# A gated cross-attention and expert layer: GpSimd's subtraction for the next batch behind the means and factors, and one gate product a step earlier

## The reference, cut to what matters

```python
xn, ln = layernorm(ctx), layernorm(layernorm(x))        # media and latents
q = ln @ Wq + bq;  k, v = split(concat(xn, ln) @ Wkv + bkv)   # 8 heads of 128
attn = softmax(q @ k.T * 128 ** -0.5)                  # 256 rows x 512 keys
x = x + tanh(g_xattn) * (attn @ v @ Wo + bo)
xh = layernorm(x)
gates = xh @ Wg + bg                                   # 8 experts, the top 2 by softmax
x = x + tanh(g_ffn) * sum over the top 2 of w_e * (silu(xh @ W1[e] + b1[e]) @ W2[e] + b2[e])
```

## Time and profile before

| | |
|---|---|
| three runs | 1504.64, 1505.71 (median), 1506.18 us |
| the profiled execution, its own time | 1498.99 us |
| its span, first to last instruction | 1497.3 us |
| TensorE busy | 1464.5 us, 98% of the span |
| VectorE busy | 1223.7 us, 82% |
| ScalarE busy | 942.0 us, 63% |
| GpSimd busy | 580.1 us, 39% |
| TensorE clock | at full speed but for the last of 40 slices |

### The profile page before, as it was taken

One profiled execution on the slowest core, in us unless ns is written; L12 is line 12 of the kernel. 1 busy time (PEld: TensorE's weight loads), 2 busy tenths in 40 slices (PEclk: granted clock), 3 DMA queues, 4 the chain that ended last, 5 costly groups with the idle time before them and its releaser, 6 DMA issues. The chain is left out here.

```text
span 1497.3 us, 29981 instructions
## 1 busy us (share of the span) xinstructions
PE 1464.5 (98%) x10138; PEld 1345.8 (90%) x10138; DVE 1223.7 (82%) x3169; ACT 942.0 (63%) x2047; POOL 580.1 (39%) x650
## 2 busy tenths in 40 slices
PE   8999999999999999999999999999999999999997
PEld 6888888888888888888988888988899999999996
DVE  7879989898898989989898998787767766666685
ACT  5665655656556555655656556556668877777775
POOL 4323324242332424324243333333444555445542
PEclk9999999999999999999999999999999999999998
DMA  6210101101110110101101010032556555555563
GB/s 200 57 36 15 43 22 41 53 16 43 23 36 22 51 43 15 44 22 46 48 16 44 23 36 22 8 98 70 111 153 195 157 132 134 145 145 128 132 184 76
DMA packets 83491, 107.99 MB, mean 72 GB/s; under 512 B 24297, under 2 KB 68390, under 8 KB 83086
## 3 DMA queue, kind: packets, MB, share of 16 engines
q1 hardware_dynamic: 67374, 87.03, 18.2%
q0 software_dynamic: 15824, 18.98, 7.9%
q10 hardware_dynamic: 144, 0.05, 0.0%
HBM read 87.68 MB, written 18.35 MB: 71 GB/s over the span
## 5 line engine op out<-in xcount | busy, mean ns | idle before, releaser
L973 POOL TENSOR_SCALAR probs<-probs,rsum 128x512 f32<-128x512 f32 x256 | 182.4, 724 | 636.2 <-DVE rsum L1696 630.1
L1197 ACT ACTIVATE pt_hi<-turn 128x512 fp32r<-128x512 f32 x256 | 139.0, 595 | 228.3 <-PE turn L1356 226.8
L999 POOL DMA_INDIRECT out_rows<-yo,token x71 | 127.6, 1797 | 188.5 <-DVE yo L1872 168.6
L1821 DVE TENSOR_TENSOR ht_lo<-hs,ht_hi 128x512 fp32r<-128x512 f32 x142 | 98.3, 692 | 116.1 <-ACT ht_hi L1164 112.9
L1096 ACT ACTIVATE probs<-score,nbias 128x512 f32<-128x512 f32 x256 | 172.8, 684 | 1.9 <-DVE nbias L1692 1.8
L1155 ACT ACTIVATE hs<-ph,vecs 128x256 f32<-128x256 f32 (+1 forms) x284 | 114.2, 457 | 94.5 <-PE ph L199 84.1
L1948 DVE TENSOR_TENSOR pt_lo<-turn,pt_hi 128x512 fp32r<-128x512 f32 x256 | 164.0, 682 | 3.9 <-ACT pt_hi L1197 3.5
L1690 DVE TENSOR_REDUCE smax<-score 128x1 f32<-128x512 f32 x256 | 164.0, 679 | 2.9 <-PE score L199 2.7
L197 PE MATMUL py<-w_hi,ht_lo 128*128 (+1 forms) x568 | 162.8, 287 | 3.2 <-DVE ht_lo L1821 1.7
L198 PE MATMUL py<-w_lo,ht_hi 128*128 (+1 forms) x568 | 161.0, 284 | 0.6 <-issue 0.5
L199 PE MATMUL py<-w_hi,ht_hi 128*128 (+1 forms) x568 | 160.8, 283 | 0.0
(11 more groups left out here) (251 smaller groups left out, 4746.5 us busy)
## 6 DMA issues: line engine op xcount, KB each, us to landing
w_raw<-in_L_ffn_W SPq DMA_DIRECT2D x45, 1024.0 KB, 5.4
spread<-mean_and_factor SPq DMA_DIRECT2D x15, 512.0 KB
xhat_rows<-rows SPq DMA_DIRECT2D x16, 264.0 KB, 2.2
x_raw<-in_x SPq DMA_DIRECT2D x16, 256.0 KB, 3.0
c_raw<-in_ctx SPq DMA_DIRECT2D x16, 256.0 KB, 3.2
out_rows<-x SPq DMA_DIRECT2D x16, 256.0 KB
z_turned<-in_x_turned SPq DMA_DIRECT2D x15, 256.0 KB, 3.8
z_turned<-in_ctx_turned SPq DMA_DIRECT2D x15, 256.0 KB, 4.5
```

Source lines behind the costliest of these rows:

```text
L973: last = pool.tensor_scalar(probs[n % 2][:, t, :], probs[n % 2][:, t, :], rsum[:, n % 2, t:t + 1], 1.0, ALU.mult, ALU.mult)
L999: pool.indirect_dma_start(out=A["out"], out_offset=bass.IndirectOffsetOnAxis(ap=token[:, u:u + 1].bitcast(U32), axis=0), in_=yo_of(t)[:, s ...
L1197: act.activation(pt[0][:, 2 * t:2 * t + 2, :], turn[t][:, :].rearrange("p (j i) -> p j i", j=2), ACT.Copy).then_inc(s_pthi, 1)
L1821: dve.tensor_tensor(lo[:, :], hs[n % N_HS][:, :], hi[:, :].bitcast(F32), ALU.subtract).then_inc(s_hlo, 1)
```

## The change

On GpSimd `split_kv` is cut in two. `round_kv` has its waits and the rounding, `rest_kv` the subtraction. In step 3 of batches 1 to 14 `round_kv` stays where `split_kv` was, and `rest_kv` comes behind `prepare`; in batch 14 and in step 4 of batch 0 nothing stands between the two. On DVE one dot of step 4, which stood ahead of the read of k, is taken away there, and step 3 gets one, which stands ahead of its read of k; the other dots of step 3 and their places count up by one. The numbers of dots are now 5, 5 and 6.

```diff
--- before.py
+++ after.py
@@ -953,15 +953,17 @@
                             in_=ids[:, TT * b + t:TT * b + t + 1], in_offset=None,
                         ).then_inc(s_listed, 16)
 
-            def split_kv(c):
+            def round_kv(c):
 
                 pool.wait_ge(s_zt, c)
                 if c >= 2:
 
                     pool.wait_ge(s_full, number["q", H * (c - 1) - 1] + 1)
                     pool.wait_ge(s_full, number["v", (2 * (c - 2) + 1, JT - 1)] + 1)
+                own.mark(pool.tensor_copy(kvt[c % 2][0][:, :, :], zt[:, :, :]))
+
+            def rest_kv(c):
                 hi, lo = kvt[c % 2]
-                own.mark(pool.tensor_copy(hi[:, :, :], zt[:, :, :]))
                 own.wait()
                 pool.tensor_tensor(lo[:, :, :], zt[:, :, :], hi[:, :, :].bitcast(F32), ALU.subtract)\
                     .then_inc(s_kvt, 1)
@@ -1015,12 +1017,16 @@
                     prepare(1)
                     routing_constants()
                 if i == 4:
-                    split_kv(1)
+                    round_kv(1)
+                    rest_kv(1)
+
 
                 if h == Z_STEP and 1 <= b < B - 1:
-                    split_kv(b + 1)
+                    round_kv(b + 1)
                 if h == A_STEP and b + 2 < B:
                     prepare(b + 2)
+                if h == Z_STEP and 1 <= b < B - 1:
+                    rest_kv(b + 1)
                 if h == R_STEP + 1 and 1 <= b < B:
                     norm_rows(b - 1)
                 if i == STEPS - 1:
@@ -1953,8 +1959,8 @@
                     lo_h(0)
                     find_places(B - 2)
                 summed = 1 <= b <= DOT_B
-                if summed and h == G_STEP:
-                    dots(b - 1, 4, 5)
+                if summed and h == T_STEP:
+                    dots(b - 1, 0, 1)
                 if summed and h == G_STEP + 1:
                     dots(b - 1, 10, 11)
                 for u in steps[i]:
@@ -1975,7 +1981,7 @@
                         if h == R_STEP + 1 and 1 <= b < B:
                             x2_moments(b - 1)
                         if summed and h == T_STEP:
-                            dots(b - 1, 0, 3)
+                            dots(b - 1, 1, 4)
                         if summed and h == G_STEP:
                             dots(b - 1, 5, 8)
                         if summed and h == G_STEP + 1:
@@ -1990,7 +1996,7 @@
                 for u in steps[i]:
 
                     if u[0] == "o" and summed and h == T_STEP:
-                        dots(b - 1, 3, 4)
+                        dots(b - 1, 4, 5)
                     if u[0] == "o" and summed and h == G_STEP:
                         dots(b - 1, 8, 9)
                     if u[0] == "o" and summed and h == G_STEP + 1:
```

## The result

The changed kernel takes 1495.2 us (median of six runs, 1494.24 to 1497.36); the kernel before, run beside it, takes 1505.18 (six runs, 1503.71 to 1506.78). The ratio is 0.9937, with a 95% interval of 0.9924 to 0.9950. Two later measurements of the same pair, on other occasions, gave 0.9949 (0.9929 to 0.9969; 1496.29 against 1504.53) and 0.9949 (0.9931 to 0.9966; 1495.58 against 1502.9). The forecast of 1497.4 was a ratio of 1497.4 / 1505.71 = 0.9945, which lies in all three intervals. By medians the change won 10.0, 8.2 and 7.3 us; 8.3 were forecast. The ratios leave out runs in a slower state (one run, of e2_dot_only) and are not the quotients of the medians; the two differ by up to 0.003.

A forecast was written before the change was run, and what follows sets the result against it. TensorE bounds the kernel, so only its standstills can be won: 13 batches times 0.64 us in step 4 = 8.3 us, other terms 0, from the median 1505.71 to 1497.4 us; range 1495.5 to 1502.5.

The forecast's parts named there:

- What bounds the kernel.: Step 4, batches 1 to 13: `nbias`, held by GpSimd's subtraction, makes the read of k late; 0.64 us reaches TensorE.
- Does the power hold `nbias`?: Step 4: `nbias` comes up inside GpSimd's moved power; no hold assumed, and one to 503.86 would still be early enough.
- "The wait of `o` is gone with the dot ahead or not: priced at 0.": Step 4: GpSimd's new order alone removes the 0.53 us lateness of `o`, so taking the dot away adds 0.
- the three dots behind the read: Step 4: DVE's dots after `kt_lo`, beside the moved subtraction, taken as held to its end; 0.75 us lost by the rule.
- The dot in step 3.: Step 3: the added 0.34 us dot fits DVE's 0.42 us idle time ahead of the read of k; cost 0.
- What is late next.: Step 5: after held dots and `rsum`, the turns' load is 0.04 us late, about 0.2 us being free; priced at 0.
- The first rival, given back in part: Chain of dots, `rsum`, scaling and turns is late beyond the 0.2 us room; 1500 to 1502 us, chance 0.16.
- "`kvt_lo`, 2 us later, is first read by the k unit of step 7.": The subtraction's output, written 2 us later in step 4, is not needed until three steps on.
- The slower rival.: Step 4: dots and subtraction take turns on SBUF, stretching the subtraction; 1506.5 us at 0.86 us stretch, 1510.9 at 1.2; chance 0.06.

The follow-up runs named there:

- e2_dot_only: Changed kernel, but GpSimd subtracts right behind the rounding as before, so only the dot is moved; 1512.28 us (1500.12 to 1522.83), ratio 1.0022.
- e9_next_step_old_dots: Changed kernel with the subtraction behind step 4's scaling of `probs` and the dots where they were before the change; 1495.78 us, ratio 0.9950.
- e1_order_only: Changed kernel with the dots put back where they were, so only GpSimd's order is new; 1512.55 us, ratio 1.0049.
- e6_three_dots_ahead: Changed kernel with three dots instead of one ahead of the read of k in step 3; 1489.93 us, ratio 0.9959.
- e4_small_twice: Changed kernel with two small GpSimd instructions of `prepare` done twice, delaying the subtraction; 1491.18 us, ratio 0.9963.
- e8_dot_behind: Changed kernel with the dot kept in step 4 but behind the read of k; 1496.3 us, ratio 0.9954.
- e3_power_twice: Changed kernel with GpSimd's power done twice, so the subtraction starts some 1.1 us later; 1508.82 us, ratio 1.0030.
- e5_next_step: Changed kernel with the subtraction one step later, behind step 4's scaling of `probs`; 1486.66 us, ratio 0.9935.
- e7_start: Changed kernel with two pieces of DVE's extra work in batch 0 each moved a step later; 1486.33 us, ratio 0.9927.
- after: The changed kernel's first measurement, against the kernel before; 1495.2 us, ratio 0.9937; its profiled execution took 1497.36 us.
- after_again: The changed kernel itself, unaltered, run again beside the first follow-up runs; 1496.29 us, ratio 0.9949.
- after_third: The changed kernel itself, unaltered, measured a third time; 1495.58 us, ratio 0.9949.
- the second group: e4_small_twice, e5_next_step, e6_three_dots_ahead and e7_start, run on another chip, where the kernel before took 1495.01 us.
- e10_next_step_start: Changed kernel with the edits of e5_next_step and e7_start together; 1494.67 us, ratio 0.9949.
- first and third group: First: e1_order_only, e2_dot_only, after_again, e3_power_twice (kernel before 1504.53 us); third: e8_dot_behind, e9_next_step_old_dots, e10_next_step_start, after_third (kernel before 1502.9 us).

## Why the prediction was right, and where a step of it was wrong

**What bounds the kernel.** Right. `nbias` held by the subtraction was the root: freed (0.17 us), step 4 is 7.90 us, 0.64 less in 13 batches, and the regular waits on `kt_lo` are gone. e9_next_step_old_dots shows it with the dots left where they were.

**Does the power hold `nbias`?** Right, and settled: it came up inside the power in the regular step 4 and took 0.17 us. One `nbias` and one dot had to bear this in the prediction; the trace of before held a second such `nbias`, in batch 0, and a dot of 0.41 us inside the power in every one of the 13 batches. The read was released by `kt_hi` 4.58 us into the step (worked out: 4.56).

**"The wait of `o` is gone with the dot ahead or not: priced at 0."** This step failed, though the forecast of the whole change came true, and it is the one from which the most is to be learned. In GpSimd's new order the dot ahead of the read would have started inside the subtraction and been held to its end. e1_order_only shows it: 2.27 us for the dot, 9.16 us for the step, 8 us lost where 8 were expected to be won. The dot's move is not worth 0 but 9.16 - 7.90 = 1.26 us a batch, 16.4 us in all (1512.55 - 1496.29 = 16.3 measured); and half the change, judged by the prediction's own working, would have been forecast with the wrong sign. What was needed stood one paragraph further on, where the three dots behind the read are taken to be held until the subtraction ends. The error was to apply this only to the instructions that stay, and to judge the one that leaves by the old order of GpSimd. That it did not hurt the sum is luck: the change happens to take away the one dot whose price was wrong.

The Trainium skill, "SBUF — State Buffer", the section on the two separate sides, says it in one sentence: a VectorE instruction with two SBUF inputs is shut out for the whole of a GpSimd instruction that reads SBUF and started first. The rows agree each time a dot met the subtraction (0.90 and 2.27 us, each ending 0.27 or 0.28 us behind it), and `pt_lo` and `kt_lo`, which take one operand from PSUM, ran beside it undisturbed (1.28 us for two, and 0.75). They do not agree for GpSimd's power, which reads SBUF as well: a dot inside it took its usual 0.41 us. There the measurement decides. And `nbias` has a single input and was held by the subtraction all the same (1.41 us), which that sentence does not cover.

**The dot in step 3.** Right: 0.34 us fits into the idle 0.42, the read starts at 497.26 as before, and e6_three_dots_ahead shows where the room ends.

**What is late next.** Right within 0.12 us. `rsum` starts 7.17 us into step 4 (worked out: 507.88 - 500.60 = 7.28), so the load is on time where 0.04 us of lateness had been forecast. The three dots lost 0.50 us (from `kt_lo` to `qt_lo` 1.53 us where it was 1.03), less than the 0.7 and 0.75 of the text; its own times, 505.83 and 507.48, make 0.62. Its 0.27 + 2 x 0.34 behind 506.6 is 507.55; 507.48 takes off the overlap of neighbours, which it doesn't say. The margin was narrow, as said: e4_small_twice and e8_dot_behind measure it at 0.15 us (worked out: 0.2). One end was not seen: with a delay of 1.1 us `qt_lo` and the scores of step 5 are late as well, ahead of the turns (e3_power_twice). The first rival, given back in part, needed some 0.2 us more delay; e8_dot_behind and e4_small_twice bring it about.

**"`kvt_lo`, 2 us later, is first read by the k unit of step 7."** Wrong, without effect: the v unit of step 5 already takes the next batch's rows, and reads `kvt_lo` some 4.4 us into step 5. The subtraction ends 5.9 us into step 4, 6.4 us ahead of that. In e5_next_step, where it ends 3.1 us into step 5, 1.3 us are left.

**The slower rival.** The dots and the subtraction did not take turns: the subtraction took 2.40 us beside the held dots, against 2.39. Its stretch in batch 0 is real (e7_start), but beside other work.

## What to carry to other kernels

When an instruction that shuts out another engine is moved, list what it newly stands beside and what it no longer does, each with its price, the instructions that another part of the change moves included: here one half alone lost 8 us, the other alone won 0.35 us a batch, and both won 0.64 us a batch. A hold costs only what exceeds the room of whoever waits behind the held instruction, so first ask which held instruction has the least room, and place the other engine's work where only the others stand.

## What the runs showed of the hardware that was not expected

**Single halts of ScalarE.** In 9 of the 14 profiled executions ScalarE stands still once for 4.5 to 6.6 us around step 0 of batch 3 (at 208 to 215 us), with no releaser on the core that the trace could name; in after:

```profile
213.19 0.60 ACT L1097 ACTIVATE v_hi<-ring 128x512 fp32r<-128x512 f32 x1 [4.72 <-remote]
```

That step took 11.8 us in after, 11.7 in after_again, 11.6 in e1_order_only, 13.6 in after_third, 10.3 in e5_next_step, 9.0 in e7_start and 8.0 in e4_small_twice. The four runs of the second group, on another chip, have no halt of this length. The kernel before has none in its one profiled execution (8.9 us), but that one is 6.2 us faster than its median, so whether the old order halts as often is not shown. e2_dot_only had a second halt. The cause is open; no experiment was made on it.

A part of the longest ones is the clock. In after_third TensorE stood still for 2.94 us during the halt, and right after that its granted clock was 0.50, which is 1.2 in place of 2.4 GHz, for 3.4 us:

```profile
215.00:218.40 3.40, 3.13 (x10) 0.50 0.00 0
```

The same fall stands at this place in e2_dot_only, e3_power_twice, e8_dot_behind, e9_next_step_old_dots and e10_next_step_start, and not in after, after_again and e1_order_only.

**A pace of 7.93 in place of 7.90 us** from batch 3 to the start of batch 14, with a granted clock of 1.00 in both, in the profiled executions of after and e1_order_only and not in those of after_again or the others: some 3 us, which is a third of what this change wins. Its cause is open too.

**Chips differ by about as much as the change.** The same kernel before took 1504.5 and 1502.9 us in the first and third group, on one chip, and 1495.0 in the second, on another. Only the ratio to a run beside it means anything at this size.
